# First layer of a four-part model on one Trainium2 core: matrix work paced by a count of TensorE columns per scan step

## The reference, cut to what matters

```python
# mixer: 16 heads of 16 keys x 16 values, one state S per head
r, k, v = xr @ Wr, xk @ Wk, xv @ Wv
g = silu(xg @ Wg); decay = exp(-exp(w0 + tanh(xw @ wA) @ wB))
def step(S, inps):                       # over all tokens of a sequence
    kv = kt[..., :, None] * vt[..., None, :]
    o = einsum('bhk,bhkv->bhv', rt, S + u[None, :, :, None] * kv)
    S = dt[..., None] * S + kv
o = (o - mean) * rsqrt(var + EPS_GN) * gn_w + gn_b      # per head
x = x + (o * g) @ Wo
x = x + gelu(rms_norm(x) @ ffn_w1) @ ffn_w2             # 256 -> 1024 -> 256
# experts: 2 shared + 16 routed, top 4 by a softmax; every expert is computed for every token
routed = sum_e gate[:, e] * (gelu(xt @ up[e]) @ down[e])
```

## Time and profile before

| | us |
|---|---|
| median of 3 runs | 5573.47 (5572.39 to 5579.07) |
| the profiled execution: its own time | 5570.63 |
| its span, first to last instruction | 5568.7 |
| mean granted TensorE clock in it | 0.898 of full |
| first layer, steady part: begin of chunk 2 to begin of chunk 15 | 322.3 to 2426.4 |

### The profile page before, as it was taken

How to read it: one execution, slowest core, us unless ns; L and a number is a source line. 1 busy time by engine, 2 the same in 40 slices (tenths; PEclk the granted TensorE clock), 3 DMA queues, 4 the chain that set the end, 5 groups by cost and what they waited for, 6 DMA issues and landing times. The chain is left out here.

```text
span 5568.7 us, 57222 instructions
## 1 busy us (share of the span) xinstructions
PE 4531.7 (81%) x18830; PEld 2929.2 (53%) x18830; DVE 4088.3 (73%) x6008; ACT 2398.5 (43%) x4532; POOL 3083.6 (55%) x1974
## 2 busy tenths in 40 slices
PE   3688888988888889888788888888888887499960
PEld 1345455555545555555445555555555555388850
DVE  4887777778877777773059999899998889354643
ACT  1233323333333233322166666666666665245530
POOL 2345444544544444453146787777787777520647
PEclk8899999999999999999898899989889997699985
DMA  3223222222322222221111111111221111386964
GB/s 114 80 91 97 91 95 85 82 99 94 97 94 90 91 80 93 93 95 65 63 43 65 68 71 60 60 58 67 75 71 68 61 56 57 139 273 221 280 191 144
DMA packets 321621, 545.14 MB, mean 98 GB/s; under 512 B 33392, under 2 KB 182000, under 8 KB 312368
## 3 DMA queue, kind: packets, MB, share of 16 engines
q1 hardware_dynamic: 293584, 465.69, 25.1%
q0 software_dynamic: 27744, 75.80, 4.2%
HBM read 422.60 MB, written 118.75 MB: 97 GB/s over the span
## 5 line engine op out<-in xcount | busy, mean ns | idle before, releaser
L1225 POOL TENSOR_TENSOR c_dbx<-c_dtx,c_Brep 128x1024 f32<-128x1024 f32 x512 | 1216.2, 2385 | 437.8 <-DVE c_hs L1243 313.6
L762 POOL TENSOR_TENSOR a_kv<-a_rkv,a_kv 128x512 f32<-128x512 f32 x512 | 762.8, 1499 | 406.4 <-DMA a_kv<-v_rows 406.2
L1243 DVE TENSOR_TENSOR_SCAN c_hs<-psum,c_carry,c_dbx 128x512 f32<-128x512 f32 x768 | 932.1, 1261 | 43.6 <-ACT psum L1232 30.6
L1259 PE MATMUL psum<-ident,c_hs 128*128 128x128 f32 x4096 | 709.6, 312 | 259.1 <-DVE c_hs L1243 249.2
L1232 ACT ACTIVATE psum<-c_dt,c_cols 128x512 f32<-128x512 f32 x1024 | 698.2, 688 | 465.3 <-DVE c_hs L1243 462.6
L1259 PEld LDWEIGHTS psum<-ident,c_hs 128*128 128x128 f32 x4096 | 543.6, 160 | 557.1 <-DVE c_hs L1243 401.0
L699 POOL TENSOR_TENSOR a_hid_e<-a_hid_e,a_g_rep 128x512 f32<-128x512 f32 x256 | 385.0, 1504 | 810.9 <-ACT a_hid_e L691 808.7
L771 DVE TENSOR_TENSOR_SCAN a_S<-a_decay,a_carry,a_kv 128x513 f32<-128x513 f32 x512 | 804.3, 1571 | 8.4 <-POOL a_kv L762 2.6
L193 PE MATMUL psum<-a_xT,a_W_up 128*128 128x512 f32 x1152 | 596.9, 646 | 54.6 <-ACT a_sq L513 37.4
L679 PE MATMUL psum<-a_W_down,a_hid_e 128*128 128x256 f32 x2304 | 548.1, 382 | 1.0 <-POOL a_hid_e L699 1.0
L679 PEld LDWEIGHTS psum<-a_W_down,a_hid_e 128*128 128x128 f32 x2304 | 445.9, 194 | 189.7 <-issue 135.1
(11 more groups left out here) (268 smaller groups left out, 7439.1 us busy)
## 6 DMA issues: line engine op xcount, KB each, us to landing
a_kv<-v_rows SPq DMA_DIRECT2D x512, 256.0 KB
a_g_rep<-g_rows SPq DMA_DIRECT2D x256, 256.0 KB, 3.4
c_Brep<-b_rows SPq DMA_DIRECT2D x64, 1024.0 KB, 4.6
d_xs<-sorted_rows SPq DMA_DIRECT2D x320, 128.0 KB
sorted_y<-d_ys SPq DMA_DIRECT2D x320, 128.0 KB
d_w<-in_d_experts SPq DMA_DIRECT2D x32, 768.0 KB, 6.1
a_xa<-in_L_attn_x SPq DMA_DIRECT2D x16, 512.0 KB, 7.1
v_rows<-a_rkv SPq DMA_DIRECT2D x16, 512.0 KB, 2.8
```

Source lines behind the costliest of these rows:

```text
L762: m_kv[g] = pool.mark(nc.gpsimd.tensor_tensor(kv[:, g % NV, 1:C + 1], rkv[slot][:, 1, hb, :], kv[:, g % NV, 1:C + 1], ALU.mult))
L1225: m_dbx[g] = m_dbx[g + 1] = pool.mark(nc.gpsimd.tensor_tensor(dbx[:, r:r + 2, :], dtx[slot][:, e, :].unsqueeze(1).broadcast_to([P, 2, C]), ...
L1243: m_scan[q] = dve.mark(nc.vector.tensor_tensor_scan(hs[:, q % NR, :], psum[:, DA + q % ND, :], dbx[:, q % NX, :], first, ALU.mult, ALU.add))
L1259: last = nc.tensor.matmul(psum[:, YB + e % 2, t * P:(t + 1) * P], hs[:, q % NR, t * P:(t + 1) * P], ident[:, :], is_transpose=True, start= ...
```

## The change

It touches the issue order of the first layer and no arithmetic.

- **Count.** `Columns.sent` counts the columns that PE streams: 2 x the width (at least 128) of each f32 product. One chunk's whole work is 150,528 columns by this count.
- **Main stream by count.** Main's rate of 1.2 is gone. After each scan step main is advanced until the columns sent since the chunk began reach 4800 times the number of steps done; 32 x 4800 = 153,600.
- **Halves.** A new `yield` lies between an up product and the down product that was issued with it, in `experts` and `feed_forward`.
- **Two streams of the chain.** `attention_out` and `expert_inputs` are streams of their own, at 2.2 each.
- **Rests.** `rest(1)` in `head_norm` and `attention_out` holds the reader of a PE result until the next scan step (in `drain`, where no step comes, it is three yields). The router's `lag` goes from 1 to 3 yields. In `attention_out` a wait in the issue order on the previous chunk's expert input is added.
- **Gates.** `experts` asks for the gates after its second up product rather than its first.

```diff
@@ -188,8 +188,14 @@
+class Columns:
+    sent = 0
 def matmuls(nc, out, pairs):
     for n, (lhsT, rhs) in enumerate(pairs):
+        Columns.sent += 2 * max(P, out.shape[1])
         last = nc.tensor.matmul(out, lhsT, rhs, start=(n == 0), stop=(n == len(pairs) - 1))
@@ -277,10 +283,18 @@
         flat = lambda ap: ap.rearrange("p a b -> p (a b)")
-        m_done, in_small = {}, []
+        m_done, in_small, now = {}, [], [0]
...
             return all(n in m_done for n in names)
+        def rest(steps):
+            until = now[0] + steps
+            for _ in range(3 * steps):
+                if now[0] >= until:
+                    break
+                yield
@@ -322,6 +336,7 @@
                     m = nc.tensor.transpose(bank[:, t * P:(t + 1) * P], src[:, t, kb * P:(kb + 1) * P], ident[:, :])
+                Columns.sent += TL * P
                 m = pe.mark(m)
@@ -491,6 +506,7 @@
                 yield
+            yield from rest(1)
             dve.after(m_done["summed", c, kb], m_done["bonus", c, kb], m_done.get(("o free", c - 1)))
@@ -498,7 +514,7 @@
             m = pe.mark(matmuls(nc, bank, [(same_head[:, :], ok)]))
-            yield
+            yield from rest(1)
             dve.after(m)
@@ -549,11 +565,13 @@
                     m_done["o free", c] = m
-                yield
+                yield from rest(1)
                 dve.after(m, m_x1)
...
             yield
+            while c >= 1 and not is_done(("xT", c - 1)):
+                yield
             act.after(m_x1, m_done.get(("hb free", c - 1)))
@@ -599,6 +618,7 @@
                                                           start=first, stop=final, skip_group_check=True)
+                        Columns.sent += 8 * D
                         m_down = m_done["hid_f free", r] = pe.mark(m_down)
@@ -629,7 +649,7 @@
             pe.after(*marks)
-            m = yield from router(nc, L, G, x_T, W_router, R, iota, 1, E, TOP)
+            m = yield from router(nc, L, G, x_T, W_router, R, iota, 1, E, TOP, 3)
             dve.after(m, m_done.get(("gates free", c - 1)))
@@ -678,8 +699,9 @@
                                                   start=(q == 0 and t % 2 == 0), stop=(q == NE - 1 and t % 2 == 1), skip_group_check=True)
+                    Columns.sent += 8 * D
                     m_down = m_done["hid_e free", r] = pe.mark(m_down)
-                if e == 0:
+                if e == SH - 1:
                     while not is_done(("gates", c)):
@@ -721,14 +743,16 @@
         steps = KB * DK
-        MAIN_RATE, CHAIN_RATE, BEFORE_RATE, NORM_RATE, LEAD = 1.2, 2.2, 1.0, 1.2, 4
+        CHAIN_RATE, BEFORE_RATE, NORM_RATE, LEAD = 2.2, 1.0, 1.2, 4
+        PACE = 4800
...
             first_chunk = chunks[0][0]
-            background = Background((MAIN_RATE, []), (CHAIN_RATE, []), (BEFORE_RATE, []), (NORM_RATE, []))
+            background = Background((0, []), (CHAIN_RATE, []), (CHAIN_RATE, []), (BEFORE_RATE, []), (NORM_RATE, []))
+            main = background.streams[0][2]
@@ -742,6 +766,7 @@
                 slot = c % 2
+                now[0] = g
                 if s == 0:
@@ -752,6 +777,7 @@
                         stream[2].extend(stages)
+                    begun = Columns.sent
                     pool.after(m_done["ready", c][0])
@@ -792,34 +818,45 @@
                                              start=(vl == 0), stop=(vl == 3), skip_group_check=True)
+                    Columns.sent += 2 * C
                     m_sum[q] = pe.mark(m)
...
                     background.pull()
+                    while main and Columns.sent - begun < PACE * (s + 1):
+                        sent = Columns.sent
+                        for _ in range(3):
+                            if main and Columns.sent == sent:
+                                background.advance(main)
+                        if Columns.sent == sent:
+                            break
             return background
...
             def prepare():
-                main, chain, ahead = [], [], []
+                main, chain, inputs, ahead = [], [], [], []
                 if c >= 1:
                     main.append(block_work(c - 2 if c >= 2 else None, c - 1))
-                    chain += [attention_out(c - 1), expert_inputs(c - 1)]
+                    chain.append(attention_out(c - 1))
+                    inputs.append(expert_inputs(c - 1))
                 if c + 1 < NCH:
...
                     ahead.append(before(c + 1))
-                return main, chain, ahead, [head_norm(c, 0)]
+                return main, chain, inputs, ahead, [head_norm(c, 0)]
             return prepare
...
         Background((1, [before(0)])).drain()
-        rest = scans([(c, stages(c)) for c in range(NCH)])
-        rest.streams[0][2].extend([block_work(last - 1, last), experts(last)])
-        rest.streams[1][2].extend([attention_out(last), expert_inputs(last)])
-        rest.drain()
+        left = scans([(c, stages(c)) for c in range(NCH)])
+        left.streams[0][2].extend([block_work(last - 1, last), experts(last)])
+        left.streams[1][2].append(attention_out(last))
+        left.streams[2][2].append(expert_inputs(last))
+        left.drain()
         L.finish()
```

## The result

The changed kernel takes 5683.9 us in the median of 4 runs (5668.6 to 5690.7); the kernel before, beside it, 5575.9 (5572.4 to 5579.1). The ratio is 1.019, 95% interval 1.0168 to 1.0212. Forecast was 5388. Each ratio leaves out runs that were longer at a lower granted clock: one of four in experiment 2 (5965.2 us, clock 0.79) and one of four in experiment 14 (5549.3, 0.87).

A forecast was written before the change was run, and what follows sets the result against it. PE was taken as nearest to full, with PE and DVE waiting for each other. Terms of -8.2 + 2 - 19.4 + 8.7 + 2.5 = -14.4 us a chunk gave 5570.6 - 187 + 2, plus 2.9: 5388 us, range 5290 to 5490.

The forecast's parts named there:

- step 2: Blocks 0 and 5 of a chunk: less PE work and rests that cut the gaps, -19.4 us a chunk.
- step 3: Blocks 6 and 7: more PE work, DVE pieces and collisions make them 35.7 us instead of 27, +8.7 a chunk.
- Step 1: Blocks 1 to 4: even columns lower PE's work to 64.5 us, -8.2 a chunk, with 2 added for block 2.
- step 4: Block 2: decay between Gelus switches ACT's table twice more and delays PE's down product, +2.5 us a chunk.
- Step 5: PE's clock, expected above 0.97; 6.8 us a chunk already inside the excesses of step 2 and step 3, nothing more counted.
- Step 6: Edges outside the 13 steady chunks: +6 us in chunk 1 and -4 at the layer's end.
- Step 7: The yield within main, later gates question and added wait in attention_out: no PE instruction, covered by main's columns.
- A: Rival: DVE takes over everywhere through collisions with POOL, chunk of 155 us, 5486 us in all; chance 0.2.
- B: Rival: banks and ACT table loads hold PE, 36 us more a chunk, 5780 us; chance 0.08 with other slowing.
- C: Rival: PE nearly full, DVE keeps up in blocks 6 and 7, chunk of 137 us, 5250 us; chance 0.1.
- D: Rival: nothing gained, the same handshakes move to other steps, 5573 us; chance 0.04.

The follow-up runs named there:

- experiment 2: The changed kernel with the next input's first-half load at scan step 20 and the second half's statistics four scan steps after its load: 5663.6 us, ratio 1.0158.
- experiment 14: 6 with 5600 columns a step instead of 4800, so the early blocks are heavy and block 6 starves: 5466.1 us, ratio 0.9807.
- 13: The changed kernel with the chunk's store of x issued from ACT's queue instead of SP's, loads left on SP: 5609.9 us, ratio 1.0066.
- 1: The changed kernel with the load of the next input's first half (a_xa) issued at scan step 20 of the chunk before: 5635.0 us, ratio 1.0119.
- 5: 1 with the statistics of the second half (a_xb) moved behind the head norm's second half, so neither load should be waited for: 5582.1 us, ratio 1.0031.
- 6: 5 with POOL's key product issued one scan step further ahead, which makes both mends on the changed kernel: 5489.4 us, ratio 0.9864.
- 8: The kernel before the change, with only POOL's key product issued one scan step further ahead: 5522.8 us, ratio 0.9928.
- 4: The changed kernel without the rests and with the router's lag back to 1: 5649.2 us, ratio 1.0143.
- 7: 5 without the rests and with the router's lag back to 1: 5525.9 us, ratio 0.9931.
- 11: The kernel before the change with both mends (early a_xa load and a_xb's statistics behind the head norm; POOL one step ahead): 5495.2 us, ratio 0.9864.

## Why the prediction was wrong, step by step

Two steps failed. Over 13 chunks the forecast was 14.4 us less a chunk, measured were 8.3 more: 22.8 us missed with the rounding. By the block means above, blocks 0 and 5 gave 6.6 us for 19.4 forecast (step 2: 12.8 missed), blocks 1 to 4 cost 3.2 instead of giving 3.7 (6.9 missed), and blocks 6 and 7 cost 11.8 for 8.7 (step 3: 3.1 missed). Step 2 is the larger in size; in step 3 a small miss in the sum hides the wait that the experiments found.

**Step 3, blocks 6 and 7: 39.7 us in chunk 9, forecast 35.7.** The size is near, the working is not. DVE was busy 24.5, not 33.7: the added pieces and collisions were over-sized by 9.2. Its idle time was 15.2 instead of 2, of which 10.75 is one wait for `a_xa`. The term that failed is "What DVE idled there, 27 - 25.2, some 2, stays": the change carries the experts' last add to the chunk's end, with it the store of `x`, and behind the store in SP's queue both loads. Shown by 13 (69 us for the store alone), 1 (40) and 5 (89, with some of PE's order). The forecast looked at the work that the change adds or moves on PE and DVE, and never at what SP's queue has waiting behind it. That the over-sized terms made up for 9.2 of the 13.2 us of idle time is luck.

**Step 2, blocks 0 and 5: 53.2 us in chunk 9, forecast 37.6, the largest miss.** The work fell to 32.6 as said, the excess rose from 17 to 20.6 instead of falling to 5. The rests did on DVE what was said of them: its wait for the scan's sum at `a_o` fell from 94.9 to 31.7 us. On PE they didn't. "I expect the gaps for a_o and part of those for a_prod to go": the wait for `a_o` rose from 43.3 to 66.9 us and that for `a_prod` from 66.7 to 83.9, while the one for `a_sq`, which was to stay, is no longer among PE's waits. "DVE may be a step ahead of PE without stopping" left POOL out. ACT, POOL, then DVE at two places, in block 0 and at its end (the last two ACT rows are a Gelu's table load and the Gelu):

```profile
1390.95 0.60 ACT L713 ACTIVATE a_hid_e<-psum 128x512 f32<-128x512 f32 x1 [2.25 <-PE psum L199]
...
1397.48 1.28 ACT L713 ACT_TABLE_LOAD   x1
1398.78 0.60 ACT L713 ACTIVATE a_hid_e<-psum 128x512 f32<-128x512 f32 x1
```

```profile
1391.63 1.26 POOL L721 TENSOR_TENSOR a_hid_e<-a_hid_e,a_g_rep 128x512 f32<-128x512 f32 x1 [4.80 <-ACT a_hid_e L713]
1392.85 1.27 POOL L788 TENSOR_TENSOR a_kv<-a_rkv,a_kv 128x512 f32<-128x512 f32 x1
...
1399.45 1.28 POOL L721 TENSOR_TENSOR a_hid_e<-a_hid_e,a_g_rep 128x512 f32<-128x512 f32 x1 [5.33 <-ACT a_hid_e L713]
```

```profile
1394.16 1.28 DVE L797 TENSOR_TENSOR_SCAN a_S<-a_decay,a_carry,a_kv 128x513 f32<-128x513 f32 x1 [4.06 <-POOL a_kv L788]
...
1401.82 2.09 DVE L797 TENSOR_TENSOR_SCAN a_S<-a_decay,a_carry,a_kv 128x513 f32<-128x513 f32 x1 [4.34 <-POOL a_kv L788]
```

POOL stands 4.80 and 5.33 us at a gate product whose Gelu is late, the key product comes behind it, and DVE's scan waits 4 us for that. At the second place the Gelu is late by ACT's own chain (Ln, Exp and their loads). At the first it had waited for PE's up product, and PE for DVE:

```profile
1383.97 2.04 PE L199 MATMUL psum<-a_o,a_same_head 128*128 128x512 f32 x2 [5.71 <-DVE a_o L511]
```

So a late `a_o` comes back to DVE through PE, ACT and POOL. That this order costs time is shown by 6 against 5: 93 us for POOL's step, with PE's wait for `a_o` down by 90. By 8 the same edit gains 40 us also where the wait is not there, so how much of the 93 is this chain isn't shown. The rests make part of it: without them DVE's wait for POOL is 118.5 for 254.7 us (4) and 184.0 for 245.5 (7), and 26 and 56 us are gained.

**Step 1, even columns.** Blocks 1 to 4 took 79.4 us for a forecast of 72.3 with the terms for block 2 and step 4. Block 1 alone has 10.5 over its 15.9 of work; the second of the places above reaches into it. Blocks 2 to 4 took 53.0 for 48.6 of work. More to the point, 6 against 11 puts the whole change at nothing, and 14 against 6 the even count at a loss of 32 us. That the starved block 6 is time lost was argued, not shown. What PE lacks there it has as backlog elsewhere. That this backlog covers waits of DVE, ACT and POOL which an even share leaves open would explain the loss, but no run shows it.

**Step 4, decay between Gelus: +2.5 forecast.** Block 2 has PE busy 18.30 of 18.30, and PE's products have no wait for `a_hid_f`'s Gelu, which the prediction named as the sign that this step is wrong: no idle time came of it.

**Step 5, clock: above 0.97 forecast.** It fell from 0.94 to 0.92, to 0.81 to 0.87 in blocks 0, 1 and 5 of chunk 9. It falls behind PE's gaps, as in block 6 before: the gap at the end of block 7 and the 5 us behind it are

```profile
1538.00:1545.00 7.00, 0.00 (x0) 0.00 (x0) 3.85 (x12) 0.00 (x0) 0.00 (x0) 0.82 0.84 231
1545.00:1550.00 5.00, 4.83 (x11) 2.65 (x12) 3.70 (x13) 0.00 (x0) 2.76 (x3) 0.57 0.23 75
```

With both mends it is 0.97 in the mean.

**Step 6, edges.** Chunk 1 took 153.1 us instead of 130.4, 22.7 more for a forecast of 6; PE's 15 us of added columns in one block were seen, that nothing elsewhere gives it back was not. The layer's end gave 13.9 for a forecast of 4. Step 7, the added `yield` and waits in the issue order, shows in no row.

**The rivals.** A is wrong: DVE is busy 118.5 us a chunk, less than before, its products at 925 ns instead of 1036. B has the sign but not the place: PE waits for the experts' Gelu 51.2 us, 3.9 a chunk, for 36 forecast; what delay the tables made arrived in part through POOL, as above. C never came up. D was closest in substance: the handshakes of router and gates did move to other places, and once both new waits were mended the changed kernel and the one before stood at the same time.

**What is left open.** Why POOL's step gains 40 us in the kernel before, with a recorded wait of 2.6; why front-loading gains 32 more; what each other part of the change is worth, since only the rests and the count were run apart. The forecast's first premise, that idle time shared by two engines is there for the taking, stands on neither.

## What to carry to other kernels

When an edit moves work to a later place, follow each queue that its last instruction releases, the issuing queue of transfers above all: a store that waits holds every load behind it, and a load whose reader comes as soon as it can land must not stand behind one. When a reader is delayed on purpose, ask which engine between the two issues something else in order behind a late operand, and put the product that the recurrence needs ahead of that. An uneven share of work isn't a loss by itself; try the mends with the old share before paying for an even one.

## What the runs showed that was not expected

The same 512 KB load took a median of 8.1 us from issue to landing in the changed kernel and 7.1 before, where it is issued at a chunk's end among the value transfers and the gates' rows (DMA engines 65% and 85% busy in block 7), 4.8 us in experiment 11, where it is issued twelve steps earlier, and 4.5 in 13, where only the store left SP's queue. A load that gets away from the other transfers is also shorter. Moving one POOL product ahead by a step changed neither its own length (1535 and 1533 ns in the median) nor any recorded wait by much, and yet it took 40 us off the kernel before.
